# A two-layer graph network: PSUM banks for the queries, a new order on TensorE, and the out-degree counts ahead of the attention loop

## The chip, the cores and the metric

The kernel runs on one core of a Trainium2 chip. The metric is the device time of one execution in microseconds (us); lower is better. TensorE is PE in the profile (its weight loads are PEld), VectorE is DVE, ScalarE is ACT, GpSimd is POOL, and SyncE, which issues the plain transfers, is SP.

## What is computed

3125 nodes with 128 features, 53125 edges sorted by their target `dst`, and 32 features for each edge. Layer 0 is an attention over the edges with 8 heads of 16; layer 1 is a graph convolution that divides by the square roots of the node degrees (in-degree plus out-degree). Cut to what matters here:

```python
Q, K, V = h @ Wq + bq, h @ Wk + bk, h @ Wv + bv        # h = relu(layernorm(x)), 8 heads
scores = sum(Q[dst] * K[src], -1) * scale + (edge_attr @ We + be)
exp_s  = exp(scores - segment_max(scores, dst)[dst])
agg    = segment_sum(exp_s * V[src], dst) / (segment_sum(exp_s, dst) + 1e-10)
x = x + agg @ Wo + bo
deg = segment_sum(1, dst) + segment_sum(1, src)        # the out-degree is the sum over src
x = x + expmap0(segment_sum(h2[src] * dinv[src] * dinv[dst], dst))
```

## The kernel before

**Stages.** First (to about 50 us) all nodes get their Q, K and V, written to tables in memory. Then the attention loop, which the change touches, takes 32 groups of 13 x 128 edges one after the other (about 60 to 971 us). After it comes layer 1, with its own loops.

**One group g of the attention loop.** POOL fetches the K and V rows of the sources, 13 indirect gathers per group into `kv[b]` (L662; two buffers, b = g mod 2). A gather of group g+2 may begin once group g has been weighed (it waits for `s_wv`). SP loads the edge features, the local target numbers `dloc_b` of the edges, spread over all partitions (L515), and a window of 128 query rows `qwin` (L530). PE selects each edge's query row by a product with a one-hot matrix `ST` (L1547): 13 tiles of 128 edges in four chunks `CH` of 4, 4, 4 and 1, into two PSUM banks `ps_q` in turn, so that chunk c waits until DVE has read chunk c-2. `ST` is made by DVE in one instruction (L872, `row_one_hots`). `bias` (L1527, L1531) adds the edge features' part in bank `ps_c`. DVE multiplies queries and keys (L927), sums per head (L933), adds the bias (L944), and then takes a segmented maximum: a scan forward inside a partition (L949), a transposition on PE (L1584), a scan over the partitions (L960), back by PE (L1587), then the same backward (L966 to L968, L1593, L979, L1595, L989 to L991). ACT takes the exponential (L1388), and DVE weighs the V rows (L1004, two instructions; each raises `s_wv`).

**Sums.** `window_sums(g)` on PE adds the weighed rows by target, 13 products with the one-hot matrix `S` (L1559, raises `s_agg`), then moves the carried rows `R` of the group before (L1565) and the carry factor (L1567, raises `s_rc`). DVE's `combine` waits for `s_rc` (L1011 to L1023), and the new rows go through `agn`, L1590, L1378 (ACT), L1600 and L1601 (PE) and L1042 to `x2`. ACT makes most of `S` (L1369 and L1372, `one_hots`), and begins on a buffer once `s_agg` says that its sums are done.

**Out-degree counts.** For each group, inside the loop, DVE makes two one-hot matrices of the sources (`oh_hi`, `oh_lo`, L897), PE multiplies them in 13 small products (L1580) into a part of bank `ps_f`, and DVE adds the result to `od_s` (`add_counts`, L904).

**What sets the order.** Every engine runs its own list of instructions in the order written; semaphores alone tie them. PE's `step(g)` is: query chunks 2 and 3 of group g, sums of group g-1, counts of g, the transpositions of g, the output product of g-1, then chunk 0, half the bias, chunk 1 and the other half of the bias of group g+1. DVE's `step(g)` is `scores(g)`, `combine(g-1)` mixed with the scan of g, the backward scan, `new_rows`, `add_counts`, `factor`, `weigh(g)`. SP waits in each turn for the stored rows of the group before the last.

## Time and profile before

| | us |
|---|---|
| median of 3 runs (1495.43 to 1497.34) | 1495.47 |
| the profiled execution, as timed | 1495.77 |
| its span, first to last instruction | 1493.8 |
| PE busy / DVE busy / ACT busy / POOL busy | 946.3 / 740.5 / 391.2 / 595.5 |
| one group of the attention loop (from its first gather at 408.49 to the next one's at 436.72) | 28.2 |

The profiled execution lies 0.3 us above the median, and 2.0 us of it lie outside the span. How to read the rows further on: a timeline row gives the start in us, the duration, the engine, the line, the operation, the tile written and the tiles read, and in brackets the idle time of the engine before it with what ended that. `<-remote` means that the profile names no instruction for the release; `<-issue` means that the engine waited for nothing that it shows. On PE a row is a time of issue, and its end is modelled. A float32 product shows as two weight loads and two matmuls, so 13 products are x26.

### The profile page before, as it was taken

What the parts mean: (1) busy time and instruction counts of PE and PEld (TensorE: products, weight loads), DVE (VectorE), ACT (ScalarE), POOL (GpSimd) and SP (SyncE); (2) the same over time, 40 slices, a digit from 0 to 9 for tenths busy, and PEclk for the clock granted to TensorE, in tenths of its full rate; (3) what the DMA queues carried; (4) which work ended last, traced back from release to release, by engine and by line L of the source; (5) the groups of instructions that cost most, each with busy time, mean ns of one, the idle gap of its engine ahead of it and who ended that gap; (6) DMA issues with size and microseconds to landing.
All of it is one profiled execution on the core that took longest, in us unless ns stands there. A gap on an engine that the chain in (4) does not pass through costs nothing.

```text
span 1493.8 us, 22198 instructions
## 1 busy us (share of the span) xinstructions
PE 946.3 (63%) x5820; PEld 805.1 (54%) x5820; DVE 740.5 (50%) x2771; ACT 391.2 (26%) x1107; POOL 595.5 (40%) x629
## 2 busy tenths in 40 slices
PE   5355775775775775675675676733757756765775
PEld 2244664664664564564564565622656645654665
DVE  8344544544554554553553553583534544454454
ACT  1502212212212212211311311142323423432341
POOL 0544454354354354354354354005343443444341
PEclk9655566566566566566566566675867877877787
DMA  5622232232232232233232233012011111111111
GB/s 150 178 80 83 87 104 82 84 104 83 81 106 86 77 110 86 72 111 89 71 112 89 70 110 93 6 47 87 26 41 34 40 40 37 37 40 40 33 41 29
DMA packets 87848, 111.23 MB, mean 74 GB/s; under 512 B 20787, under 2 KB 65791, under 8 KB 87807
## 3 DMA queue, kind: packets, MB, share of 16 engines
q0 software_dynamic: 26624, 68.20, 15.8%
q1 hardware_dynamic: 61191, 42.64, 9.9%
q8 instruction: 15, 0.25, 0.1%
q14 instruction: 18, 0.15, 0.0%
HBM read 99.83 MB, written 10.95 MB: 74 GB/s over the span
## 4 chain that ended last, share of the span: by engine, by line
PE 33%; DVE 24%; issue 20%; another core or an unknown queue 19%; DVEq 2%; DMA 1%; SPq 0%; ACT 0%
PE ps_q L1547 10%; PE ps_q L1673 3%; PE ps_q L1698 3%; PE ps_s L1673 3%; PE ps_c L1531 3%; DVE sc L933 2%; DVE wv L1275 2%; PE ps_f L1601 2%; PE ps_f L1600 1%; DVE fwd_reset L1274 1%; DVE prod L927 1%; PE ps_c L1527 1%; DVE oh_lo L897 1%; PE ps_b L1673 1%
## 5 line engine op out<-in xcount | busy, mean ns | idle before, releaser
L662 POOL DMA_INDIRECT kv<-kv_tab,idx x416 | 396.6, 953 | 533.8 <-DVE wv L1004 367.6
L695 POOL DMA_INDIRECT kv<-hs_tab,idx x208 | 198.6, 955 | 335.9 <-PE ps_q L1682 191.6
L1369 ACT ACTIVATE S<-iota,nloc 128x128 f32<-128x128 f32 x384 | 122.0, 389 | 636.1 <-remote 635.0
L1547 PE MATMUL ps_q<-qwin,ST 128*128 128x128 f32 x832 | 207.0, 432 | 19.5 <-DVE prod L927 10.5
L1547 PEld LDWEIGHTS ps_q<-qwin,ST 128*128 128x128 f32 x832 | 187.1, 331 | 20.8 <-DVE prod L927 10.8
L1580 PE MATMUL ps_f<-oh_lo,oh_hi 128*50 128x64 bf16 x416 | 83.4, 301 | 96.2 <-issue 96.0
L927 DVE TENSOR_TENSOR prod<-kv,ps_q 128x512 f32<-128x512 f32 (+1 forms) x128 | 74.6, 583 | 140.2 <-issue 58.8
L1011 DVE TENSOR_SCALAR fb<-ps_c 128x8 f32<-128x8 f32 x32 | 5.3, 166 | 274.3 <-remote 267.3
L1559 PE MATMUL ps_r<-wv,S 128*128 128x137 f32 x832 | 140.1, 341 | 1.8 <-DVE wv L1004 1.8
L1559 PEld LDWEIGHTS ps_r<-wv,S 128*128 128x128 f32 x832 | 140.0, 253 | 2.1 <-DVE wv L1004 2.1
L1580 PEld LDWEIGHTS ps_f<-oh_lo,oh_hi 128*50 128x50 bf16 x416 | 54.2, 172 | 110.4 <-issue 109.4
L1689 PE MATMUL ps_r<-qkv,xt 128*128 128x128 f32 x800 | 95.5, 280 | 5.6 <-issue 5.4
L1689 PEld LDWEIGHTS ps_r<-qkv,xt 128*128 128x128 f32 x800 | 93.6, 196 | 7.6 <-issue 7.6
L1673 PE MATMUL ps_q<-ST,wv 128*128 128x128 bf16 x224 | 48.4, 300 | 63.4 <-issue 47.2
L1587 PE MATMUL ps_b<-ident,c 8*128 8x8 f32 x32 | 7.7, 241 | 127.5 <-DVE c L960 127.5
L1587 PEld LDWEIGHTS ps_b<-ident,c 8*128 8x128 f32 x32 | 5.6, 176 | 142.3 <-issue 142.3
L1673 PE MATMUL ps_s<-ST,wv 128*128 128x128 bf16 x224 | 48.0, 304 | 45.0 <-issue 45.0
L1448 ACT ACTIVATE S<-iota,nloc 128x128 f32<-128x128 f32 x208 | 67.0, 387 | 26.0 <-PE ps_q L1682 26.0
L1531 PEld LDWEIGHTS ps_c<-we,attr_s 128*128 128x128 f32 (+1 forms) x256 | 63.0, 321 | 19.9 <-DMA attr_s<-in_attr 12.1
L1531 PE MATMUL ps_c<-we,attr_s 128*128 128x32 f32 (+1 forms) x256 | 65.8, 378 | 11.8 <-DMA attr_s<-in_attr 11.8
L933 DVE TENSOR_REDUCE sc<-prod 128x32 f32<-128x512 f32 (+1 forms) x128 | 71.5, 579 | 0.0
L1673 PEld LDWEIGHTS ps_q<-ST,wv 128*128 128x128 bf16 x224 | 26.6, 135 | 75.2 <-issue 65.1
(257 smaller groups left out, 1715.6 us busy)
## 6 DMA issues: line engine op xcount, KB each, us to landing
dloc_b<-dloc_tab SPq DMA_DIRECT2D x32, 416.0 KB
kv<-kv_tab,idx POOLq DMA_INDIRECT x416
attr_s<-in_attr SPq DMA_DIRECT2D x32, 192.0 KB
kv<-hs_tab,idx POOLq DMA_INDIRECT x208
kv_tab<-qkv SPq DMA_DIRECT2D x5, 640.0 KB, 4.0
x_tab<-x SPq DMA_DIRECT2D x32, 64.5 KB, 1.7
qwin<-q_tab SPq DMA_DIRECT2D x32, 64.0 KB
xwin<-in_x SPq DMA_DIRECT2D x32, 64.0 KB
```

The source lines that it names most:

```text
L662: pool.indirect_dma_start(out=kv[:, b, t, :], out_offset=None, in_=kv_tab, in_offset=bass.IndirectOffsetOnAxis(ap=idx[:, b, t:t + 1], axis ...
L695: pool.indirect_dma_start(out=kv[:, j, t, 0:D], out_offset=None, in_=hs_tab, in_offset=bass.IndirectOffsetOnAxis(ap=idx[:, j, t:t + 1], ax ...
L927: V.tensor_tensor(prod[:, c % 2, 0:w, :], kv[:, b, t0:t1, 0:D], ps_q[c % 2][:, 0:w * D].rearrange("p (t d) -> p t d", d=D), ALU.mult).then ...
L933: st.mark(V.tensor_reduce(sc[:, :, t0:t1].rearrange("p h t -> p t h"), prod[:, c % 2, 0:t1 - t0, :].rearrange("p t (h d) -> p t h d", d=DH ...
L1369: A.activation(S[:, b, t, :], iota[:], ACT.Abs, bias=nloc[:, g, t:t + 1] if known(g) else nloc[:, bass.ds(g, 1), t:t + 1].rearrange("p g t ...
L1448: A.activation(S[:, j, t, :], iota[:], ACT.Abs, bias=nloc[:, g, t:t + 1] if known(g) else nloc[:, bass.ds(g, 1), t:t + 1].rearrange("p g t ...
L1531: mm = M.matmul(p_bias[:, 4 * H * k:4 * H * k + w], attr_s[0:r, b, k, :], we4[0:r, 0:w], start=False, stop=k == 3)
L1547: mm = M.matmul(ps_q[c % 2][:, (t - t0) * D:(t - t0 + 1) * D], ST[:, b, t, :], qwin[:, b, :], start=True, stop=True)
L1559: mm = M.matmul(ps_r[:, 0:C + 1], S[:, b, t, :], wv[:, t, :], start=(t == 0), stop=(t == T - 1))
L1580: mm = M.matmul(ps_f[0:HI, 3 * D:3 * D + LO], oh_hi[:, b, :, t], oh_lo[:, b, :, t], start=(t == 0), stop=(t == T - 1))
L1673: mm = M.matmul(bank[:, 0:(h1 - h0) * P].rearrange("p (h e) -> p h e", e=P) [:, :, ROW0[t]:ROW0[t] + W], oh_node[:, t, :], oh_key(t)[:, h0 ...
L1689: M.matmul(ps_r[:, 0:D], counts[:, i, :], hs_t[:, i, :], start=(i == 0), stop=False)
```

## The change

- **PSUM.** Four banks hold the four query chunks, `ps_q[0]` to `ps_q[3]`; the old `ps_s` banks are the last two of them. The bias moves into the free part of `ps_q[3]`. A chunk now waits only until DVE has read the same chunk of the group before.
- **PE's order.** `step(g)` begins with the sums of group g-1. The four query chunks of group g+1 stand between and behind the transpositions of g: chunk 0 after L1584's transposition, chunk 1 after the one of `agn`, chunk 2, the whole bias and chunk 3 after the output product.
- **`ST` moves from DVE to ACT.** In place of one DVE instruction, ACT makes two of the same size, the absolute difference and then relu(1 - it), one group earlier than before. SP loads `dloc_b` a group earlier, too.
- **Counts.** The counts of all 32 groups are made before the attention loop, in one PSUM accumulation in bank `ps_r`, and DVE copies the result once. `source_one_hots` and the 13 products leave the loop, and so does `add_counts`.
- **ACT's order.** The third part of `one_hots` goes behind the exponential.

```diff
-        ps_q = [pb(f"ps_q{i}", [P, 512]) for i in range(2)]
-        ps_s = [pb(f"ps_s{i}", [P, 512]) for i in range(2)]
+        ps_q = [pb(f"ps_q{i}", [P, 512]) for i in range(NCH)]
+        ps_s = ps_q[2:]
...
-        p_bias = ps_c[:, 384:384 + HT]
+        p_bias = ps_q[NCH - 1][:, D:D + HT]
+        p_od = ps_r[0:HI, 2 * D:2 * D + LO]
...
-                    wait_apart(sp, s_st, g - 1, (s_base, 1))
+                    wait_apart(sp, s_sta, g - 1, (s_base, 1))
...
-                load_dloc(g, b)
...
+                load_dloc(0, 0)
+                load_dloc(1, 1)
                 load_edges(0, 0)
                 load_edges(1, 1)
+                load_dloc(2, 0)
...
-                with sp.Fori(1, GROUPS // 2) as n:
-                    for b in range(2):
-                        load_edges(2 * n + b, b)
-                        store_nodes(2 * n + b - 2, b)
-                        load_nodes(2 * n + b, b)
+
+                def turn(g, b, more=True):
+                    if more:
+                        load_dloc(g + 1, 1 - b)
+                    load_edges(g, b)
+                    store_nodes(g - 2, b)
+                    load_nodes(g, b)
+
+                with sp.Fori(1, GROUPS // 2 - 1) as n:
+                    turn(2 * n, 0)
+                    turn(2 * n + 1, 1)
+                turn(GROUPS - 2, 0)
+                turn(GROUPS - 1, 1, more=False)
                 store_nodes(GROUPS - 2, 0)
-                sp.wait_ge(s_od, GROUPS)
+                sp.wait_ge(s_od, 1)
...
-            def row_one_hots(g, b):
-
-                dve.wait_ge(s_dlocb[b], 16 * ((g - b) // 2 + 1) if known(g) else (g + (2 - b)) * 8)
-                if not (known(g) and g < 2):
-                    dve.wait_ge(s_qt, NCH * (g - 1))
-                V.tensor_scalar(ST[:, b].rearrange("p t e -> p (t e)"), dloc_b[:, b, :], imj[:, 0:1], None, ALU.is_equal)\
-                    .then_inc(s_st, 1)
...
-            pre.mark(V.memset(od_s[:], 0.0))
             dve.wait_ge(s_reset8, 2 * H)
             dve.wait_ge(s_line, 16)
-            def source_one_hots(g, b, parts=(0, 1)):
-
-                if 0 in parts and not (known(g) and g < 2):
+            def source_one_hots(g, b):
+
+                if not (known(g) and g < 2):
                     dve.wait_ge(s_hist, g - 1)
-                for i in parts:
+                for i in range(2):
...
-            def add_counts(g):
-                dve.wait_ge(s_hist, g + 1)
-                if not (known(g) and g == 0):
-                    dve.wait_ge(s_od, g)
-                V.tensor_tensor(od_s[:], od_s[:], ps_f[0:HI, 3 * D:3 * D + LO], ALU.add).then_inc(s_od, 1)
...
-                if more:
-                    source_one_hots(g + 1, 1 - b, (0,))
...
-                if more:
-                    source_one_hots(g + 1, 1 - b, (1,))
...
-                    row_one_hots(g + 2, b)
...
-                    add_counts(g)
...
-            source_one_hots(0, 0)
...
-                row_one_hots(0, 0)
+                source_one_hots(0, 0)
+                source_one_hots(1, 1)
+                with dve.Fori(1, GROUPS // 2) as n:
+                    source_one_hots(2 * n, 0)
+                    source_one_hots(2 * n + 1, 1)
+                dve.wait_ge(s_hist, GROUPS)
+                V.tensor_copy(od_s[:], p_od).then_inc(s_od, 1)
...
+            def row_one_hots(g, b):
+
+                act.wait_ge(s_dlocb[b], 16 * ((g - b) // 2 + 1) if known(g) else (g + (2 - b)) * 8)
+                if not (known(g) and g < 2):
+                    act.wait_ge(s_qt, NCH * (g - 1))
+                rows = ST[:, b].rearrange("p t e -> p (t e)")
+                A.activation(rows, dloc_b[:, b, :], ACT.Abs, bias=nrow[:]).then_inc(s_sta, 1)
+                act.wait_ge(s_sta, g + 1)
+                A.activation(rows, rows, ACT.Relu, bias=1.0, scale=-1.0).then_inc(s_st, 1)
...
-            def step(g, b, nodes=True, more=True):
+            def step(g, b, nodes=True, more=True, far=True):
+                if far:
+                    row_one_hots(g + 2, b)
                 if more:
-                    one_hots(g + 1, 1 - b, (0, 1))
+                    one_hots(g + 1, 1 - b, (0,))
...
-                    one_hots(g + 1, 1 - b, (2,))
+                    one_hots(g + 1, 1 - b, (1,))
...
-            act.wait_ge(s_nloc, 1)
+                if more:
+                    one_hots(g + 1, 1 - b, (2,))
+
+            act.wait_ge(s_nloc, 2)
...
+                row_one_hots(0, 0)
+                row_one_hots(1, 1)
                 step(0, 0, nodes=False)
-                with act.Fori(0, GROUPS // 2 - 1) as n:
+                step(1, 1)
+                with act.Fori(1, GROUPS // 2 - 1) as n:
+                    step(2 * n, 0)
                     step(2 * n + 1, 1)
-                    step(2 * n + 2, 0)
-                step(GROUPS - 1, 1, more=False)
+                step(GROUPS - 2, 0, far=False)
+                step(GROUPS - 1, 1, more=False, far=False)
...
-                    if c == chunks[0]:
+                    if c == 0:
                         pe.wait_ge(s_st, g + 1)
-                    if not (known(g) and g == 0 and c < 2):
-                        pe.wait_ge(s_prod, NCH * g + c - 1)
+                    if not (known(g) and g == 0):
+                        pe.wait_ge(s_prod, NCH * (g - 1) + c + 1)
                     for t in range(t0, t1):
-                        mm = M.matmul(ps_q[c % 2][:, (t - t0) * D:(t - t0 + 1) * D], ST[:, b, t, :], qwin[:, b, :],
+                        mm = M.matmul(ps_q[c][:, (t - t0) * D:(t - t0 + 1) * D], ST[:, b, t, :], qwin[:, b, :],
                                       start=True, stop=True)
                     mm.then_inc(s_qt, 1)
-            def window_sums(g, b, bias_read=True):
+            def histogram(g, b):
+
+                pe.wait_ge(s_oh, 2 * g + 2)
+                for t in range(T):
+                    mm = M.matmul(p_od, oh_hi[:, b, :, t], oh_lo[:, b, :, t],
+                                  start=known(g) and g == 0 and t == 0, stop=known(g) and g == GROUPS - 1 and t == T - 1)
+                mm.then_inc(s_hist, 1)
+
+            def window_sums(g, b):
...
-                if bias_read:
-                    pe.wait_ge(s_sc, g + 2)
...
+                if nodes:
+                    window_sums(g - 1, 1 - b)
                 if edges:
-                    query(g, b, (2, 3))
-                if nodes:
-                    window_sums(g - 1, 1 - b, edges)
-                if edges:
-
-                    pe.wait_ge(s_oh, 2 * g + 2)
-                    if not (known(g) and g == 0):
-                        pe.wait_ge(s_od, g)
-                    for t in range(T):
-                        mm = M.matmul(ps_f[0:HI, 3 * D:3 * D + LO], oh_hi[:, b, :, t], oh_lo[:, b, :, t],
-                                      start=(t == 0), stop=(t == T - 1))
-                    mm.then_inc(s_hist, 1)
                     pe.wait_ge(s_v1, g + 1)
                     M.transpose(p_v1, f1[:, :, T - 1], ident[:]).then_inc(s_v1T, 1)
-                if edges:
+                    if more:
+                        query(g + 1, 1 - b, (0,))
...
+                    if more:
+                        query(g + 1, 1 - b, (1,))
...
-                    query(g + 1, 1 - b, (0,))
-                    bias(g + 1, 1 - b, (0, 1))
-                    query(g + 1, 1 - b, (1,))
-                    bias(g + 1, 1 - b, (2, 3))
+                    query(g + 1, 1 - b, (2,))
+                    bias(g + 1, 1 - b, (0, 1, 2, 3))
+                    query(g + 1, 1 - b, (3,))
...
+                histogram(0, 0)
+                histogram(1, 1)
+                with pe.Fori(1, GROUPS // 2 - 1) as n:
+                    histogram(2 * n, 0)
+                    histogram(2 * n + 1, 1)
+                histogram(GROUPS - 2, 0)
+                histogram(GROUPS - 1, 1)
+                pe.wait_ge(s_od, 1)
                 bias(0, 0, (0, 1, 2, 3))
-                query(0, 0, (0, 1))
+                query(0, 0, (0, 1, 2, 3))
```

How this moves the instructions: on PE, in the steady part of the loop, before (`ps_q0` and `ps_q1` are the two query banks, L1559 the sums, L1580 the counts, L1587 to L1593 transpositions):

```order
L1547 MATMUL ps_q0<-qwin,ST 128x128 x4
L1545 REGISTER_ALU
L1547 MATMUL ps_q1<-qwin,ST 128x128
L1553 REGISTER_ALU
L1554 REGISTER_ALU
L1559 MATMUL ps_r<-wv,S 128x137 x13
L1565 MATMUL ps_c<-R,shift 128x137
L1567 MATMUL ps_c<-facd,isf 128x8
L1576 ISA
L1580 MATMUL ps_f<-oh_lo,oh_hi 50x64 x13
L1584 MATMUL ps_b<-ident,f1 8x128
L1587 MATMUL ps_b<-ident,c1 128x8
```

The counts stand between the sums and the first transposition, and the query chunks ahead of the sums. The same place after the change (the sums are L1581, the queries L1561, the transposition of `c1` is L1598):

```order
L1581 MATMUL ps_r<-wv,S 128x137 x13
L1585 MATMUL ps_c<-R,shift 128x137
L1587 MATMUL ps_c<-facd,isf 128x8
L1593 REGISTER_ALU
L1594 MATMUL ps_b<-ident,f1 8x128
L1553 ISA
L1559 ISA
L1561 MATMUL ps_q0<-qwin,ST 128x128 x4
L1598 MATMUL ps_b<-ident,c1 128x8
L1601 MATMUL ps_f<-ident,agn 128x128
L1559 REGISTER_ALU
L1561 MATMUL ps_q1<-qwin,ST 128x128 x4
```

The counts are gone, and chunks 0 and 1 of the next group now stand among the transpositions. On DVE, in `combine`, before (L1011 reads the product of L1567, L872 makes `ST`, L1023 adds the sums):

```order
L1011 TENSOR_SCALAR fb<-ps_c 128x8
L1012 COPY R<-ps_c 128x1
L860 TENSOR_SCALAR shift<-imj,delta 128x128
L1016 TENSOR_TENSOR R<-ps_c,fb 128x136
L864 TENSOR_TENSOR S<-dloc,iota 128x128
L872 TENSOR_SCALAR ST<-dloc_b,imj 128x1664
L1023 TENSOR_TENSOR R<-R,ps_r 128x137
```

And after:

```order
L1006 TENSOR_SCALAR fb<-ps_c 128x8
L1007 COPY R<-ps_c 128x1
L874 TENSOR_SCALAR shift<-imj,delta 128x128
L1011 TENSOR_TENSOR R<-ps_c,fb 128x136
L878 TENSOR_TENSOR S<-dloc,iota 128x128
L1017 TENSOR_TENSOR R<-R,ps_r 128x137
```

The instruction that made `ST` has left the path from the release of `combine` to the addition.

## Rows read from the trace of the kernel before

**Rows 1.** Head of the page: span.

```profile
span 1493.8 us, 22198 instructions
```

**Rows 2.** Waits, 90 to 1000 us: total us, times, longest us.

```profile
ACT S L1369 <- remote: 635.0, 30, 21.4
POOL kv L662 <- DVE wv L1004: 367.6, 30, 17.0
DVE fb L1011 <- remote: 267.3, 30, 9.3
```

**Rows 3.** Timeline, one group of the attention loop, 408 to 428 us.

```profile
408.49 0.95 POOL L662 DMA_INDIRECT kv<-kv_tab,idx  x1 [12.11 <-DVE wv L1004]
...
414.13 4.10 PE L1559 MATMUL ps_r<-wv,S 128*128 128x137 f32 x26
...
418.39 0.38 PE L1567 MATMUL ps_c<-facd,isf 8*128 8x8 f32 x2
...
422.67 0.28 PE L1580 MATMUL ps_f<-oh_lo,oh_hi 128*50 128x64 bf16 x1 [1.06 <-issue]
...
423.37 0.28 PE L1580 MATMUL ps_f<-oh_lo,oh_hi 128*50 128x64 bf16 x1 [0.42 <-issue]
...
423.59 0.95 POOL L662 DMA_INDIRECT kv<-kv_tab,idx  x1 [0.30 <-issue]
...
427.08 0.17 DVE L1011 TENSOR_SCALAR fb<-ps_c 128x8 f32<-128x8 f32 x1 [8.81 <-remote]
427.14 1.28 ACT L1369 ACTIVATE S<-iota,nloc 128x128 f32<-128x128 f32 x4 [21.27 <-remote]
```

**Rows 4.** Timeline, the same group after the release, 427 to 437 us.

```profile
427.83 1.08 DVE L872 TENSOR_SCALAR ST<-dloc_b,imj 128x1664 f32<-128x1664 bf16 x1
...
431.26 0.38 PE L1593 MATMUL ps_b<-ident,bx 128*8 128x128 f32 x1 [0.49 <-DVE bx L968]
...
433.77 1.92 PE L1547 MATMUL ps_q<-qwin,ST 128*128 128x128 f32 x8
...
434.48 0.20 DVE L904 TENSOR_TENSOR od_s<-od_s,ps_f 50x64 f32<-50x64 f32 x1
...
435.62 0.75 PE L1527 MATMUL ps_c<-be_r,ones_row 1*128 1x104 f32 x2
...
436.30 1.06 PE L1531 MATMUL ps_c<-we,attr_s 128*128 128x32 f32 x4
...
436.72 0.94 POOL L662 DMA_INDIRECT kv<-kv_tab,idx  x1 [12.18 <-DVE wv L1004]
```

**Rows 5.** Timeline, group 31's step, in which no gather runs, 948 to 954 us.

```profile
948.66 4.76 PE L1559 MATMUL ps_r<-wv,S 128*128 128x137 f32 x26
...
954.00 0.17 DVE L1011 TENSOR_SCALAR fb<-ps_c 128x8 f32<-128x8 f32 x1 [2.26 <-PE ps_c L1567]
```

**Rows 6.** Timeline, the step of group 1, 99 to 118 us.

```profile
99.40 0.94 POOL L662 DMA_INDIRECT kv<-kv_tab,idx  x1 [17.00 <-DVE wv L1004]
...
115.80 1.28 ACT L1369 ACTIVATE S<-iota,nloc 128x128 f32<-128x128 f32 x4 [18.41 <-remote]
...
117.86 0.17 DVE L1011 TENSOR_SCALAR fb<-ps_c 128x8 f32<-128x8 f32 x1 [9.34 <-remote]
```

**Rows 7.** Timeline, the start of the attention loop, 58 to 99 us.

```profile
58.86 0.52 DVE L897 TENSOR_TENSOR oh_hi<-hi_f,rep_hi 128x650 bf16<-128x650 bf16 x1 [8.15 <-ACT bwd_reset L1407]
59.30 0.61 DVE L897 TENSOR_TENSOR oh_lo<-lo_f,rep_hi 128x832 bf16<-128x832 bf16 x1
...
81.45 0.95 POOL L662 DMA_INDIRECT kv<-kv_tab,idx  x1 [0.30 <-issue]
...
86.42 0.69 DVE L927 TENSOR_TENSOR prod<-kv,ps_q 128x512 f32<-128x512 f32 x1 [11.95 <-remote]
...
87.89 1.76 PE L1580 MATMUL ps_f<-oh_lo,oh_hi 128*50 128x64 bf16 x13
...
97.42 1.96 DVE L1004 TENSOR_TENSOR wv<-kv,wv 128x1024 f32<-128x1024 f32 x2 [0.20 <-ACT wv L1388]
```

More of the change, by code:

```diff
@@ L185, in build @@
         dloc_b = sb("dloc_b", [P, 2, GE], BF16)
+        nrow = sb("nrow", [P, 1])
         lo_f = sb("lo_f", [P, GROUPS, T], BF16)
@@ L359, in build @@
         s_stp = sem("s_stp")
+        s_sta = sem("s_sta")
         s_st = sem("s_st")
@@ L843, in _ @@
             V.tensor_scalar(nloc[:], dloc[:], -1.0, None, ALU.mult).then_inc(s_nloc, 1)
+            V.tensor_scalar(nrow[:], imj[:, 0:1], -1.0, None, ALU.mult).then_inc(s_nloc, 1)
             V.tensor_scalar(part_reset[:], part_reset[:], BIG, None, ALU.mult).then_inc(s_part, 1)
@@ L916, in mask8, with scores @@
                 return col3(tile, g).unsqueeze(1).to_broadcast([P, H, T])
-            def scores(g, b, st, more):
+            def scores(g, b, st):
                 def product(c):
@@ L927, in product @@
                     V.tensor_tensor(prod[:, c % 2, 0:w, :], kv[:, b, t0:t1, 0:D],
-                                    ps_q[c % 2][:, 0:w * D].rearrange("p (t d) -> p t d", d=D), ALU.mult).then_inc(s_prod, 1)
+                                    ps_q[c][:, 0:w * D].rearrange("p (t d) -> p t d", d=D), ALU.mult).then_inc(s_prod, 1)
                 def per_head(c):
@@ L1055, in step @@
                 if edges:
-                    scores(g, b, A, more)
+                    scores(g, b, A)
                 if nodes:
@@ L1064, in step @@
                     edge_one_hots(g + 1, 1 - b, s_S, TA)
-                    row_one_hots(g + 1, 1 - b)
                 if edges:
```

## The prediction

> **What bounds the kernel now.** I read the list of waits first, then the timeline of one group of the attention loop, then the places where that pattern is broken. The waits [rows 2] show three engines that stand still together: POOL for 367.6 us until a group is weighed, and ACT for 635.0 us and DVE for 267.3 us on a release that no instruction accounts for ("remote"). One group shows where these lie [rows 3]. POOL's 13 gathers run from 408.49 to 424.54, and PE issues the sums at 414.13 and the carry product L1567 at 418.39, modelled to end at 418.77. DVE's `combine` reads that product, yet it starts at 427.08, and ACT, which waits for the sums, at 427.14. Meanwhile PE issues its small products one at a time, 0.70 us apart (422.67, 423.37). So what PE has finished reaches the others some 8.3 us late, and it reaches them 18.6 us after the first gather (408.49 to 427.08), 2.5 us after the last one has ended.
>
> Two other places say on what this hangs. In group 31's step no gather runs, and DVE starts 5.3 us after the sums do, not 12.9 us [rows 5]. In the step of group 1 ACT was released 16.4 us and DVE 18.5 us after the first gather [rows 6]: the release can come a little before the gathers end, but not much. I conclude that a step is a loop of two legs. **Leg 1** runs from the first gather to the release of `combine`, 18.6 us, and its length is that of the gathers. **Leg 2** runs from the release through the scans to the weighing, which lets POOL begin the next gathers: 427.08 to 436.72 [rows 3, 4], 9.6 us. Together 28.2 us, 31 times, some 875 of the span of 1493.8 us [rows 1]. Work inside leg 1 is covered; work in leg 2, or ahead of the loop, is paid.
>
> **Part 1: the counts ahead of the loop.** Inside the loop they are nearly free: the two one-hots (0.52 and 0.61 us [rows 7]) and the 13 products lie in leg 1, and only the addition L904 (0.20 us [rows 4]) lies in leg 2. Moved ahead they are all on the path, since bias, queries and the first step now stand behind them on PE and DVE. Without gathers 13 such products take 1.76 us with the modelled end of the last [rows 7]; I take 1.6 us per group, more than DVE's 1.13 us. The first gathers run until 82.4 (81.45 + 0.95), and PE's releases were held until 86.42 [rows 7], and DVE idled 11.95 us on a remote release there. So I let only 2 of the 32 groups through by 86.4, and the other 30 end at 86.4 + 30 x 1.6 = 134.4. Then come the bias (0.75 + 2 x 1.06 = 2.9 us) and two query chunks (2 x 1.92) [rows 4], so DVE's second product starts at 141.1. From there to the first weighing it was 97.42 - 86.42 = 11.0 us [rows 7], which I keep: 152.1 in place of 97.42, **+54.7 us**. The ends: if nothing is held, the counts start at 59.4 and end at 110.6, which gives +30.9; with no group through by 86.4 and 1.76 us each, +63.
>
> **Part 2: `ST` goes to ACT.** L872 (1.08 us [rows 4]) leaves DVE in leg 2. ACT does two instructions of that size. The widest ACT row at hand is four one-hots in 1.28 us, 512 columns [rows 3]; by columns 1664 come to 4.2 us each at most, 8.3 us for two, against some 21 us in which ACT idles before L1369 [rows 3]. They are used a group later. I cost them at nothing; were they in leg 2, they would cost up to 8 us a group, but the order puts them ahead of the wait for the sums. SP's earlier `dloc_b` moves a transfer inside leg 1 and is not waited for.
>
> **Part 3: PE's new order.** Chunk 0 (1.92 us [rows 4]) now stands behind the transposition of `f1`. In leg 1 PE can issue it while the others wait, so it costs nothing. Chunk 1 is issued behind the transposition of `agn`, which comes in leg 2, and right ahead of the transposition L1593 on which DVE waits: +1.92 us, less the 0.49 us that PE idled there, less what L872's going gives back. So leg 2 changes by +1.92 - 0.49 - 1.08 - 0.20 = +0.15 us; the ends are -1.28 (if chunk 1 is hidden entirely) and +0.64 (if PE's idle time takes up none of it). I take **0 +- 5 us** for the loop; over 31 steps the ends are -40 and +20. Chunk 2, the bias and chunk 3 follow the output product (1.92 + 2.9 + 0.5 = 5.3 us, chunk 3 being one tile of 13). From chunk 0 of before at 433.77 that is 439.1, so that the sums start 2.4 us after the first gather (436.72 [rows 4]) in place of 5.6 us (408.49 to 414.13 [rows 3]).
>
> **Do the sums then get through?** This decides. Between the first gather and the sums PE had before the change chunk 1 (8 passes), part of the bias, and chunks 2 and 3 (10), some 22 passes; now it has most of the bias and chunk 3, some 9. That is some 13 passes fewer, and 3.2 us. But 3.2 us earlier is not enough, if the rate of the reports is what is short: at 0.70 us for one, 12 us of leg 1 carry 17. ACT's 7 instructions have come into leg 1 as well. I take it that the release still comes with the end of the gathers.
>
> A release is prompt where nothing disturbs it: in [rows 5] it is 5.3 us from the first sum, all 30 passes included. The Trainium skill, "TensorE: Matmul & The Clock Gate", section "The cost: per-tile semaphore tail", puts one increment some 56 ns behind its matmul. By that rule `combine` would start at 418.8 in place of 427.08, and the loop after the change would be the third rival below; the trace disagrees by 8.3 us while gathers run.
>
> **Sum:** 1495.8 (the profiled execution) + 54.7 + 0 = 1550.5, and 0.3 less against the median: **1550 us**.
>
> **Rivals.** *First, faster: the release comes before the gathers end.* Mechanism: with fewer passes ahead of it, `s_rc` reaches DVE by, say, 14 us after the first gather; `combine` and the scan of L960 run under the gathers, and at their end only the backward part is left. It decides if the release comes more than 1 us before the 18.6 us. For it: [rows 6], where ACT was released at 16.4 us, with no transfers by SP in that stretch. Against it: the whole of what follows needs further reports. Price: of the 4.2 us from L1011 to L1593 (427.08 to 431.26 [rows 3, 4]) some 3 us, 30 times 3 = 90: 1550 - 90 = 1460; with all 4.2 us, 1424.
>
> *Second, slower: PE cannot issue chunk 0 under cover.* Then it runs in leg 2, ahead of the transposition of `c1`: 1.92 x 31 = 60, 1610 us. For it: in [rows 3] PE issues its small products only 0.70 us apart while the others wait, as if its queue were full. Against it: it still advances by one every 0.70 us, and chunk 0 has 8 passes and over 9 us. The Trainium skill, same page, section "Architectural detail: the array is 16x 32x32, not 1x 128x128", gives TensorE a queue of 64; sums, carry, `f1` and chunk 0 make 78 entries by it, so 14 would have to be freed first. The trace agrees in so far as the issue slows down in that stretch, and at 0.70 us each the 14 are freed within leg 1, so the forecast has no price for it.
>
> *Third, much faster: the lateness goes away altogether*, because it hung on the order of PE's work and not on the gathers. Then the sums start 2.4 us after the first gather, the release follows 5.3 us later [rows 5], and leg 2 takes its 9.6 us: 17.3 us a step, just over the 16.4 us of 13 gathers (408.49 to 424.54 and one pause of 0.30 [rows 3]). 31 x 10.9 = 338 saved: 1212. Against it: POOL would then gather without a break, and releases are late just while it gathers.
>
> **Chances.** Forecast 0.60 (its own range 1515 to 1575), first rival 0.21, second 0.11, third 0.08. The range reaches down to the middle of the first rival, 1440, and up to 1590; left out are the third, the second and the far end of the first, about 0.2. A measurement of this kernel tells 0.2%, 3 us, from no change. Faster: 0.29; slower: 0.60 and 0.11 less a little, 0.69; within 0.2%: 0.02.
>
> **What would show it.** In the profile after: the last count product at about 134 us and the first L1004 at about 152; a step of the loop still 28 us, with DVE's first instruction of `combine` released by "remote" 18 to 19 us after the first gather; chunk 1 in 1.9 us ahead of the transposition of `bx`. The forecast is wrong if the step is 25 us or less (the release was not tied to the gathers, or got through early), or if the counts end before 115 (the hold did not apply to them).

## Result: slower by 2.2% in the recorded comparison, faster by 5.8% in another

| | before | after |
|---|---|---|
| median (runs) | 1495.45 us (4) | 1527.86 us (4, 1524.74 to 1533.82) |
| the profiled execution, as timed | 1495.77 | 1524.91 |
| its span | 1493.8 | 1523.1 |

The ratio is 1.0222, with a 95% interval of 1.0193 to 1.025: slower, clear of noise, and by about 2%. 1550 us was forecast, with a range of 1440 to 1590.

The experiments then met a second condition of the hardware, which has to be told first, because every number below depends on it. The delay of PE's releases that [rows 3] show is not always there. The kernels were run on several occasions, each time together with the kernel before. On some occasions the kernel before takes 1495 to 1511 us and PE's releases come late while POOL gathers. On others the same kernel takes 1043 to 1044 us and they come at once. All runs of one occasion, those of the kernel before among them, agreed in this. I call the two **with the delay** and **without**; comparisons of times hold inside one occasion only. The recorded comparison is one with the delay. Without it the unaltered changed kernel takes 984.15 us beside 1044.06 us (below).

**The profile after, with the delay.** The list of waits, 90 to 1000 us (total us, times, longest us), answers [rows 2]:

```profile
POOL kv L675 <- DVE wv L999: 406.3, 30, 70.4
DVE fb L1006 <- remote: 350.9, 28, 13.5
...
ACT S L1365 <- remote: 172.4, 28, 10.7
```

DVE waits longer for the release of `combine` than before (350.9 us for 267.3 us), since it comes to that wait earlier. ACT waits less (172.4 us for 635.0 us), since it now makes `ST` and waits for its input, and since what it waits for is released earlier, as the group below shows. The first row holds one wait of 70.4 us: POOL stands still during the counts. The start of the loop in the timeline (start, duration, in brackets the idle time before) answers [rows 7]:

```profile
59.31 0.52 DVE L902 TENSOR_TENSOR oh_hi<-hi_f,rep_hi 128x650 bf16<-128x650 bf16 x1 [9.42 <-issue]
...
80.70 0.95 POOL L675 DMA_INDIRECT kv<-kv_tab,idx  x1 [0.30 <-issue]
...
85.69 0.52 DVE L902 TENSOR_TENSOR oh_hi<-hi_f,rep_hi 128x650 bf16<-128x650 bf16 x1 [18.62 <-remote]
...
86.79 45.17 PE L1569 MATMUL ps_r<-oh_lo,oh_hi 128*50 128x64 bf16 x377 [17.90 <-DVE oh_lo L902]
...
132.00 0.22 DVE L1172 COPY od_s<-ps_r 50x64 f32<-50x64 f32 x1 [1.93 <-PE ps_r L1569]
...
137.07 0.69 DVE L926 TENSOR_TENSOR prod<-kv,ps_q 128x512 f32<-128x512 f32 x1 [4.86 <-PE ps_q L1561]
...
150.06 1.96 DVE L999 TENSOR_TENSOR wv<-kv,wv 128x1024 f32<-128x1024 f32 x2 [0.33 <-ACT wv L1394]
```

DVE stands still for 18.62 us in the middle of the counts, until 4.0 us after the last of the first gathers has ended, as forecast. 29 of the 32 groups (377 = 29 x 13 products) follow it. The first weighing is at 150.06 in place of 97.42. A group in the loop, beside [rows 3] and [rows 4]:

```profile
785.98 0.94 POOL L675 DMA_INDIRECT kv<-kv_tab,idx  x1 [11.96 <-DVE wv L999]
...
788.33 5.77 PE L1581 MATMUL ps_r<-wv,S 128*128 128x137 f32 x26
...
790.75 1.68 ACT L1376 ACTIVATE ST<-dloc_b,nrow 128x1664 f32<-128x1664 bf16 x1 [5.50 <-DMA dloc_b<-dloc_tab]
...
792.46 1.59 ACT L1378 ACTIVATE ST<-ST 128x1664 f32<-128x1664 f32 x1
...
794.26 0.38 PE L1587 MATMUL ps_c<-facd,isf 8*128 8x8 f32 x2
...
800.28 1.28 ACT L1365 ACTIVATE S<-iota,nloc 128x128 f32<-128x128 f32 x4 [6.22 <-remote]
...
801.00 0.94 POOL L675 DMA_INDIRECT kv<-kv_tab,idx  x1 [0.30 <-issue]
...
804.39 0.17 DVE L1006 TENSOR_SCALAR fb<-ps_c 128x8 f32<-128x8 f32 x1 [13.29 <-remote]
...
806.88 1.91 PE L1561 MATMUL ps_q<-qwin,ST 128*128 128x128 f32 x8
...
808.58 0.42 PE L1606 MATMUL ps_b<-ident,bx 128*8 128x128 f32 x1
...
813.95 0.95 POOL L675 DMA_INDIRECT kv<-kv_tab,idx  x1 [12.00 <-DVE wv L999]
```

The sums start 2.35 us after the first gather, in place of 5.64 us, and the carry product is issued 8.3 us after it, in place of 9.9 us. DVE gains almost nothing by it: `combine` starts 18.4 us after the first gather, where it was 18.6 us. The product is now almost 10 us old when DVE learns of it. ACT does gain. It waits for the sums alone, which PE issues just ahead of the carry product, and starts at 800.28, 14.3 us after the first gather and with one gather still to come. In the kernel before it started together with DVE, 18.7 us after the first gather (427.14 in [rows 3]). But ACT is not on the path. Leg 2 is 9.56 us (804.39 to 813.95), where it was 9.64 us.

**Where the time went**, by the weighings of the groups in both timelines (their first and last, 97.42 and 961.12 before, 150.06 and 988.91 after). The counts cost 52.6 us ahead of the loop. The loop is 24.9 us shorter: 10.8 us in 27 steady steps (0.4 each), 3.2 us in the first step and 10.8 us in the last three. Layer 1 is 1.5 us longer. 52.6 - 24.9 + 1.5 = 29.2 us; the spans, 1493.8 and 1523.1, differ by 29.3, which is rounding. In the first and the last steps the release did come before the end of the gathers. The last burst:

```profile
951.26 0.95 POOL L675 DMA_INDIRECT kv<-kv_tab,idx  x1 [9.57 <-DVE wv L999]
...
963.36 0.17 DVE L1006 TENSOR_SCALAR fb<-ps_c 128x8 f32<-128x8 f32 x1 [6.99 <-remote]
...
966.31 0.95 POOL L675 DMA_INDIRECT kv<-kv_tab,idx  x1 [0.31 <-issue]
```

12.1 us after the first gather, while the last gather still starts at 966.31.

### The profile page after: what moved, and what is told of

Same layout as the page of the kernel before. It is cut to its first block, busy times and chain, and to the rows that moved or that the text cites. A ratio compares the mean times of both kernels' runs of the same rounds, so it can differ in the third digit from the quotient of the medians.

```text
span 1523.1 us, 22133 instructions
## 1 busy us (share of the span) xinstructions
PE 904.4 (59%) x5820; PEld 793.5 (52%) x5820; DVE 708.6 (47%) x2708; ACT 499.1 (33%) x1171; POOL 595.3 (39%) x629
## 4 chain that ended last, share of the span: by engine, by line
another core or an unknown queue 26%; DVE 26%; PE 25%; issue 17%; DVEq 2%; DMA 1%; ACT 1%; SPq 0%; ACTq 0%
PE ps_q L1693 6%; PE ps_q L1561 4%; DVE sc L932 3%; PE ps_r L1569 3%; PE ps_q L1718 3%; DVE wv L999 3%; DVE prod L926 2%; DVE wv L1271 2%; PE ps_f L1614 2%; DVE fwd_reset L1270 2%; PE ps_f L1613 1%; DVE ST L1270 1%; PE ps_r L1581 1%; PE ps_f L1601 1%
## 5 line engine op out<-in xcount | busy, mean ns | idle before, releaser
L1598 PE MATMUL ps_b<-ident,c 8*128 8x8 f32 x32 | 7.7, 239 | 314.2 <-DVE c L955 296.3
L1006 DVE TENSOR_SCALAR fb<-ps_c 128x8 f32<-128x8 f32 x32 | 5.3, 166 | 384.2 <-remote 350.9
L1365 ACT ACTIVATE S<-iota,nloc 128x128 f32<-128x128 f32 x384 | 122.1, 389 | 184.9 <-remote 172.4
L1561 PE MATMUL ps_q<-qwin,ST 128*128 128x128 f32 x832 | 181.2, 382 | 0.0
L1598 PEld LDWEIGHTS ps_b<-ident,c 8*128 8x128 f32 x32 | 5.6, 175 | 319.4 <-issue 319.4
L1561 PEld LDWEIGHTS ps_q<-qwin,ST 128*128 128x128 f32 x832 | 163.0, 287 | 0.8
L1581 PE MATMUL ps_r<-wv,S 128*128 128x137 f32 x832 | 160.0, 374 | 1.8 <-DVE wv L999 1.8
L1581 PEld LDWEIGHTS ps_r<-wv,S 128*128 128x128 f32 x832 | 159.9, 284 | 2.0 <-DVE wv L999 2.0
L1376 ACT ACTIVATE ST<-dloc_b,nrow 128x1664 f32<-128x1664 bf16 x32 | 53.8, 1682 | 230.2 <-DMA dloc_b<-dloc_tab 138.3
L1693 PE MATMUL ps_q<-ST,wv 128*128 128x128 bf16 x448 | 61.3, 302 | 105.4 <-issue 92.3
L1693 PEld LDWEIGHTS ps_q<-ST,wv 128*128 128x128 bf16 x448 | 46.0, 136 | 124.7 <-issue 108.9
L1569 PE MATMUL ps_r<-oh_lo,oh_hi 128*50 128x64 bf16 x416 | 50.3, 299 | 35.9 <-DVE oh_lo L902 32.5
L1474 ACT COPY xt<-ps_q 128x512 f32<-128x512 f32 x64 | 32.9, 600 | 117.2 <-PE ps_q L1693 105.1
L1569 PEld LDWEIGHTS ps_r<-oh_lo,oh_hi 128*50 128x50 bf16 x416 | 49.5, 170 | 36.6 <-DVE oh_lo L902 33.0
```

Of the source, the lines that this page charges most:

```text
L1365: A.activation(S[:, b, t, :], iota[:], ACT.Abs, bias=nloc[:, g, t:t + 1] if known(g) else nloc[:, bass.ds(g, 1), t:t + 1].rearrange("p g t ...
L1376: A.activation(rows, dloc_b[:, b, :], ACT.Abs, bias=nrow[:]).then_inc(s_sta, 1)
L1561: mm = M.matmul(ps_q[c][:, (t - t0) * D:(t - t0 + 1) * D], ST[:, b, t, :], qwin[:, b, :], start=True, stop=True)
L1569: mm = M.matmul(p_od, oh_hi[:, b, :, t], oh_lo[:, b, :, t], start=known(g) and g == 0 and t == 0, stop=known(g) and g == GROUPS - 1 and t ...
L1581: mm = M.matmul(ps_r[:, 0:C + 1], S[:, b, t, :], wv[:, t, :], start=(t == 0), stop=(t == T - 1))
L1693: mm = M.matmul(bank[:, 0:(h1 - h0) * P].rearrange("p (h e) -> p h e", e=P) [:, :, ROW0[t]:ROW0[t] + W], oh_node[:, t, :], oh_key(t)[:, h0 ...
```

## Experiments

### First occasion: the counts, and SP's loads (without the delay)

The kernel before took 1043.92 us here (13 runs), not 1495 us. This is where the second condition showed itself; no expectation written for this occasion had foreseen it, so their times are not met.

**Part 1 alone**, in the kernel before:

```diff
-                    add_counts(g)
+                source_one_hots(0, 0)
...
+                dve.wait_ge(s_hist, GROUPS)
+                V.tensor_copy(od_s[:], p_od).then_inc(s_od, 1)
```

> The kernel before with part 1 alone: the counts ahead of the loop, PE's and ACT's order and the banks as before. After the change the first weighing came 52.6 us later (97.42 to 150.06), and that should repeat here. Theory 'end of the gathers' (the release of `combine` comes 18.5 us after the first gather whatever is queued): the loop loses only the addition L904, 31 x 0.2 = 6 us; in all 1495.5 + 52.6 - 6 = 1542 us. Theory 'shared' (while gathers run, the instructions that all engines have in that stretch hold one another up, so that fewer of them release `combine` earlier): the counts stood behind the carry product on PE, but two one-hots of DVE and 26 weight loads and products leave the stretch; the release should move to 15 to 18 us, and the time to 1460 to 1530 us.

Measured: 1094.04 us, ratio 1.0481 (1.0463 to 1.0498).

**The counts left out** of the kernel before (no one-hots of the sources, no products, no addition; zeros in `od_s`):

> The kernel before, the out-degree counts left out altogether (zeros instead). It prices what the counts cost inside the loop. 'End of the gathers': 0.2 us a group, 1495.5 - 6 = 1489 us. 'Shared': the release comes at 15 to 18 us in place of 18.5, and the time is 1410 to 1480 us.

Measured: 1043.53 us, ratio 0.9996 (0.9986 to 1.0005). So the counts inside the loop cost nothing that can be measured, not even the 6 us of the additions, and the two runs together price the phase ahead of the loop at 50.5 us. Its timeline shows one step of the old order without the delay:

```profile
427.42 0.94 POOL L662 DMA_INDIRECT kv<-kv_tab,idx  x1 [3.61 <-DVE wv L1000]
...
433.19 4.73 PE L1553 MATMUL ps_r<-wv,S 128*128 128x137 f32 x26
...
438.09 0.38 PE L1561 MATMUL ps_c<-facd,isf 8*128 8x8 f32 x2
...
438.51 0.17 DVE L1007 TENSOR_SCALAR fb<-ps_c 128x8 f32<-128x8 f32 x1 [2.08 <-PE ps_c L1561]
...
448.21 0.94 POOL L662 DMA_INDIRECT kv<-kv_tab,idx  x1 [4.37 <-DVE wv L1000]
```

`combine` starts 0.42 us after the issue of the carry product, not 8.7 us after it as in [rows 3], with the same order of instructions up to there and the same gathers beside it. What bounds the step here is a chain through PE: query chunks, sums, `combine`, scans, weighing, 20.5 us on the average, and POOL waits some 4 us in each.

**The counts back in the loop** of the changed kernel, parts 2 and 3 kept:

```diff
+                    add_counts(g)
...
-                histogram(0, 0)
...
+                    for t in range(T):
+                        mm = M.matmul(ps_f[0:HI, 3 * D:3 * D + LO], oh_hi[:, b, :, t], oh_lo[:, b, :, t],
```

> The changed kernel with the counts put back into the loop, as before the change (the one-hots behind the scores, the 13 products behind the sums, an addition a group), parts 2 and 3 kept. The 52.6 us ahead of the loop go. 'End of the gathers': 1527.9 - 52.6 + 6 = 1481 us. 'Shared': the 28 additional instructions push every release back to 18.5 us, and the early releases of the first and last steps (9.9, 14.9 and 12.1 us) are lost, so the loop gives back most of the 25 us it had won: 1490 to 1505 us.

Measured: 955.90 us, ratio 0.9186 (0.9125 to 0.9247). Parts 2 and 3 are worth 8.1% without the delay.

**SP's loads left out** from group 2 on, in the changed kernel (the data of groups 0 and 1 are used again, so the scores are not the reference's):

> The changed kernel without SP's loads of dloc_b, attr_s and qwin for groups 2 to 31 (the data of groups 0 and 1 are used again). In the changed kernel the release of `combine` came 17.0 to 18.5 us after the first gather where SP made all its loads, 14.9 and 12.1 us in the last two bursts of gathers, where it made fewer, and 9.9 us in the first, where it made none. 'End of the gathers': no change, 18.5 us, 1528 us. 'Shared' or 'SP's transfers': some 15 of SP's instructions and 4 transfers fewer in each burst, release at 10 to 14 us, step 23 to 25 us, 1400 to 1450 us.

Measured: 983.98 us, ratio 0.9422 (0.9404 to 0.9441). It says nothing on the delay, since there was none; beside the next run it says that the loads cost nothing without it.

### Second occasion: the changed kernel itself (without the delay)

> The changed kernel unaltered, beside the kernel before. In the first four runs the kernel before took 1044 us in place of 1495 us, and PE's releases came without delay. If the comparison is again one without the delay: the counts ahead of the loop cost 1094.0 - 1043.5 = 50.5 us, so 955.9 + 50.5 = 1006 us against 1044 us, faster by 3.6%. If it is one with the delay: 1528 us against 1495 us, and the theories 'end of the gathers' and 'shared' both expect that.

Measured: 984.15 us beside 1044.06 us, ratio 0.9421 (0.939 to 0.9452). 1006 us was expected from the price of the phase; it is 22 us less, because the loop of the changed kernel without the counts is also shorter than with them (weighing to weighing 523.7 us for 543.9 us). The waits of 150 to 600 us:

```profile
POOL kv L675 <- issue: 102.3, 336, 0.3
DVE prod L926 <- DMA kv<-kv_tab,idx: 96.4, 39, 4.9
```

POOL waits for nothing but its own pause of 0.3 us between two gathers, and DVE waits for gathered rows. The step of 17.07 us (groups 2 to 28) is that of 13 gathers, a few of which take longer than the usual 0.95 us (2.39 us below). In the timeline of one step:

```profile
386.44 0.38 PE L1587 MATMUL ps_c<-facd,isf 8*128 8x8 f32 x2
...
388.16 0.69 DVE L926 TENSOR_TENSOR prod<-kv,ps_q 128x512 f32<-128x512 f32 x1 [3.36 <-DMA kv<-kv_tab,idx]
...
391.39 0.14 DVE L1006 TENSOR_SCALAR fb<-ps_c 128x8 f32<-128x8 f32 x1
...
399.78 2.39 POOL L675 DMA_INDIRECT kv<-kv_tab,idx  x1 [0.30 <-issue]
...
402.47 0.94 POOL L675 DMA_INDIRECT kv<-kv_tab,idx  x1 [0.30 <-issue]
```

The carry product is issued 5 us before DVE comes to it, so sums that stood on the path before the change stand beside it now.

**ACT's first part of `S` behind the copy of `agT`,** and its second behind the exponential:

```diff
-                if more:
-                    one_hots(g + 1, 1 - b, (0,))
                 if nodes:
                     agg_copy(g - 1)
                 if more:
-                    one_hots(g + 1, 1 - b, (1,))
+                    one_hots(g + 1, 1 - b, (0,))
                 carry_factor(g)
                 weights(g)
                 if more:
-                    one_hots(g + 1, 1 - b, (2,))
+                    one_hots(g + 1, 1 - b, (1, 2))
```

> The changed kernel with ACT's first part of the one-hots `S` moved behind the copy of `agT`, so that ACT runs nothing between the sums and the release of `combine`. Without the delay: within 1% of the changed kernel, since ACT has idle time. With it: 'end of the gathers' expects the release at 18.5 us as in the changed kernel, 'shared' expects it at 13 to 16 us, as the five instructions of ACT no longer stand between the sums and the carry product.

Measured: 985.73 us (2 runs), no difference from the changed kernel. What it was made for, the delay, was not there.

### Third occasion: parts 2 and 3 undone one at a time (with the delay, before 1507.57 us)

**`ST` on DVE again:**

```diff
+                if far:
+                    row_one_hots(g + 3, 1 - b)
```

> The changed kernel with `ST` made by DVE's one instruction again (behind the one-hots `S` in `combine`, still a group ahead), so part 2 alone undone. Without the delay of PE's releases the changed kernel took 984 us and its step 17.07 us, which is the gathers' own 13 x 1.25 us and a short pause. If the gathers bound the step (third rival of the prediction), 1.1 us more on DVE is mostly covered: 984 to 995 us. If DVE's path bounds it, 31 x 1.1 = 34 us: 1018 us.

Measured: 1575.89 us, ratio 1.0454 (1.0433 to 1.0475). A step of it, in the timeline:

```profile
672.24 0.94 POOL L675 DMA_INDIRECT kv<-kv_tab,idx  x1 [13.25 <-DVE wv L1007]
...
690.91 0.17 DVE L1014 TENSOR_SCALAR fb<-ps_c 128x8 f32<-128x8 f32 x1 [13.63 <-remote]
...
691.66 1.08 DVE L886 TENSOR_SCALAR ST<-dloc_b,imj 128x1664 f32<-128x1664 bf16 x1
...
701.35 0.95 POOL L675 DMA_INDIRECT kv<-kv_tab,idx  x1 [13.16 <-DVE wv L1007]
```

**PE's queries and bias where they stood before:**

```diff
+                    query(g, b, (2, 3))
                 if nodes:
                     window_sums(g - 1, 1 - b)
...
-                        query(g + 1, 1 - b, (1,))
```

> The changed kernel with PE's query chunks and the bias where they stood before the change (chunks 2 and 3 ahead of the sums, 0 and 1 behind the output product), the four banks, `ST` on ACT and the counts ahead kept, so part 3's order alone undone. Without the delay: if the order is what shortened the step from 20.5 to 17.1 us, it returns to 19 to 20.5 us, since the product of chunk 2 waits for PE in the stretch behind the weighing: 1045 to 1080 us. If the banks or `ST` did it: 984 to 1000 us.

Measured: 1524.66 us, ratio 1.0113 (1.0093 to 1.0133):

```profile
640.12 0.94 POOL L675 DMA_INDIRECT kv<-kv_tab,idx  x1 [11.28 <-DVE wv L999]
...
658.87 0.17 DVE L1006 TENSOR_SCALAR fb<-ps_c 128x8 f32<-128x8 f32 x1 [8.16 <-remote]
...
667.27 0.95 POOL L675 DMA_INDIRECT kv<-kv_tab,idx  x1 [11.24 <-DVE wv L999]
```

In both the release of `combine` stays near where it was, 18.7 us after the first gather (672.24 to 690.91, 640.12 to 658.87), for 18.4 us in the changed kernel. Leg 2 changes: 10.44 us with `ST` on DVE and 8.40 us with the old order on PE. It is 0.1 us longer in every second step, so these two go with the 9.46 us of the changed kernel's next step (832.42 to 841.88) and not with the 9.56 us above. So `ST`'s going gave 1.0 us a step, and chunk 1 on the path took 1.1 us of it back. The expectations of these two runs were written for the other condition, so their numbers are not met.

The old order of PE also shows what the new one does to the releases. With it ACT is released 18.4 to 18.9 us after the first gather in every burst (18.8 us in the step above), with the new one, in the changed kernel, after 12.2 to 15.1 us in all steady steps but one (16.4 us). For `combine` this counts mainly at the ends of the loop: in the first and the last three steps the new order is 9.4 us shorter in all, in the 27 others it is 14.5 us longer (27.75 us a step for 27.21 us). The loop is 838.8 us with the new order and 833.7 us with the old one. So with the delay part 3 is a small loss. The ratios to the kernel before (1.0113 without it, 1.0222 with it) say the same, but they come from two occasions, and layer 1, which is the same in both kernels, differs by 5.9 us between them (540.1 us for 534.2 us). How the 3.4 us a step that parts 2 and 3 bring without the delay divide between them was not measured.

### Fourth and fifth occasion: a version that beats both, and fewer gathers

**The counts hidden in the loop:** the changed kernel with the counts back in the loop, their DVE part ahead of the product of chunk 2:

```diff
+                    if c == 1:
+                        if not (known(g) and g == 0):
+                            add_counts(g - 1)
+                        if more:
+                            source_one_hots(g + 1, 1 - b)
                     if c + 1 < NCH:
                         product(c + 1)
```

> A version that may beat both: the changed kernel with the counts in the loop, the 13 products behind the sums on PE, and DVE's one-hots and the addition of the counts put ahead of the product of chunk 2, where DVE waits for the gathered rows. Without the delay: the loop keeps the changed kernel's step of 17.1 us and loses the 47 us ahead of it: 984 - 47 = 937 us, against 956 us with the one-hots behind the scores. With the delay: 'end of the gathers' expects 1481 us, 'shared' 1490 to 1505 us, before 1495 us.

Measured without the delay: 939.87 us beside 1043.79 us, ratio 0.8997 (0.8968 to 0.9027). 937 us was expected. In its timeline the three instructions stand where DVE would wait for rows, and the wait that is left there is 0.60 us:

```profile
307.96 0.20 DVE L910 TENSOR_TENSOR od_s<-od_s,ps_f 50x64 f32<-50x64 f32 x1
308.08 0.51 DVE L903 TENSOR_TENSOR oh_hi<-hi_f,rep_hi 128x650 bf16<-128x650 bf16 x1
308.52 0.60 DVE L903 TENSOR_TENSOR oh_lo<-lo_f,rep_hi 128x832 bf16<-128x832 bf16 x1
...
309.72 0.69 DVE L933 TENSOR_TENSOR prod<-kv,ps_q 128x512 f32<-128x512 f32 x1 [0.60 <-DMA kv<-kv_tab,idx]
```

The step is 17.06 us, that of the changed kernel, with the first weighing at 82.50. The same kernel on the fifth occasion:

> The version with the counts hidden in the loop once more, for the other condition of the chip if it shows. With the delay: no counts phase ahead (-52.6 us), the step of the changed kernel, at most 0.3 us more: 1528 - 53 + 0 to 10 = 1475 to 1485 us against 1495 us of before. Without it: 940 us against 1044 us, as measured.

Measured with the delay: 1496.22 us beside 1510.56 us, ratio 0.9908 (0.9886 to 0.9931). It beats the kernel before under both conditions, here by 0.9%. The time expected, 1475 to 1485 us, was not met. The kernel before itself took 15 us more than in the recorded comparison. And the loop takes 856.7 us in place of the changed kernel's 838.8: none of its 27 steady steps has an early release (all 18.55 to 18.78 us after the first gather), where the changed kernel has seven. So with the delay the counts do not seem free in the loop (17.9 us between these two traces, which are of two occasions), but cheaper than ahead of it (the first weighing comes at 99.29 in place of 150.06).

**Six gathers of 13** from group 2 on, in the changed kernel (the other tiles keep old rows, so the sums are not the reference's):

```diff
+FEW = (2, 2, 1, 1)
...
-                    for t in range(t0, t1):
+                    for t in range(t0, t1 if known(g) else t0 + FEW[c]):
```

> The changed kernel with 6 of the 13 gathers of each group from group 2 on (the other tiles keep the rows of groups 0 and 1). If PE's releases are delayed (the kernel before at about 1500 us): the last gather then ends 5 x 1.255 + 0.95 = 7.2 us after the first, and if the release hangs on the end of the gathers, `combine` starts 9.6 us after the first gather in place of 18.5 us, the step falls to about 19 us, and layer 1 stays as it is: 1250 to 1270 us. If the delay has nothing to do with the gathers, 1528 us stays. If nothing is delayed (before at 1044 us): the step of 17.07 us was the gathers', so it falls to the path of DVE, which is busy about 15 us a step: 984 less 31 x 1.5 to 2 us, 920 to 940 us.

Measured with the delay: 1225.62 us beside 1510.56 us, ratio 0.8116 (0.806 to 0.8171). The expected 1250 to 1270 us are missed by 24 us, since the step is 17.3 us and not 19. The first three rows are of one of three bursts inside the loop in which the carry product comes early, the others of a usual one:

```profile
304.86 0.94 POOL L676 DMA_INDIRECT kv<-kv_tab,idx  x1 [9.57 <-DVE wv L1000]
...
308.27 0.38 PE L1588 MATMUL ps_c<-facd,isf 8*128 8x8 f32 x2
...
313.63 0.17 DVE L1007 TENSOR_SCALAR fb<-ps_c 128x8 f32<-128x8 f32 x1 [3.64 <-remote]
...
426.81 0.94 POOL L676 DMA_INDIRECT kv<-kv_tab,idx  x1 [10.14 <-DVE wv L1000]
...
433.05 0.95 POOL L676 DMA_INDIRECT kv<-kv_tab,idx  x1 [0.30 <-issue]
...
433.80 0.38 PE L1588 MATMUL ps_c<-facd,isf 8*128 8x8 f32 x2
...
435.62 0.17 DVE L1007 TENSOR_SCALAR fb<-ps_c 128x8 f32<-128x8 f32 x1 [3.80 <-PE ps_c L1588]
...
444.35 0.94 POOL L676 DMA_INDIRECT kv<-kv_tab,idx  x1 [10.36 <-DVE wv L1000]
```

The release follows the gathers: it comes 8.8 us after the first (9.6 us expected) in place of 18.4 us, 1.6 us after the last has ended, and 1.8 us after the issue of the carry product where it was 10 us. That it hangs on the gathers and not on the product is seen where the product is issued at 308.27, 3.4 us after the first gather: the release comes 8.8 us after the gather there, too. So with the delay the gathers set the length of leg 1, as the prediction had it.

**What holds it while they run** is open. The theory "shared" (the number of instructions of all engines in the burst) does not order the early releases: counted up to the release, the last bursts held 142 instructions (12.1 us, changed kernel), 145 (17.2 us, `ST` on DVE) and 173 (12.2 us, counts hidden). SP's transfers order them only in part. In the three kernels with PE's new order the first burst has none of them, and it released after 9.9, 10.0 and 5.9 us; the last has fewer than elsewhere (12.1, 17.2 and 12.2 us). But the last burst but one has all of them and released after 14.9, 18.7 and 17.3 us. And with PE's old order the first burst, with no transfer of SP, released only after 18.5 us, in the kernel before [rows 6] and in the run with the old order alike. There the sums are issued 5.2 us after the first gather, in the three others at most 1.8 us after it. So what is issued early in a burst gets through early, at least at the ends of the loop. That is not all either: ACT's releases in the steady steps come after 12.2 to 16.4 us in the changed kernel, after 15.8 to 18.8 us with `ST` on DVE and after 12.3 to 18.7 us with the counts hidden, all three with the new order. No run takes these apart. The last run, on a sixth occasion, was to decide on SP's transfers:

> The changed kernel without SP's loads of dloc_b, attr_s and qwin for groups 2 to 31 once more (the data of groups 0 and 1 are used again). So far, with the delay, a burst of gathers in which SP makes none of its transfers released `combine` after 5.9 to 10.0 us, one with fewer after 12.1 to 17.3 us, all others after 17.0 to 18.8 us, in three kernels; the number of instructions of all engines does not order them (173 in the burst that took 12.2 us, 142 in the one that took 12.1 us, 145 in the one that took 17.2 us). If SP's transfers beside the gathers carry the delay, every burst releases after 6 to 10 us, and the step falls to 17 to 20 us: 1190 to 1290 us beside about 1500 us of before. If the end of the gathers alone carries it, 18.5 us and about 1530 us stay. If nothing is delayed in this run, 984 us as before, and the question stays open.

Measured: 985.86 us beside 1043.32 us, so without the delay, and the question stays open as that text says.

## Why the prediction was right, and where it was not

**Part 1** held. 54.7 us were forecast, 52.6 us came. The hold until the end of the gathers ended at 85.69 (86.42 assumed), 3 groups were through by then (2 assumed), and the others took 45.17 / 29 = 1.56 us each (1.6 assumed). Without the delay nothing is held: on the second occasion the counts run in one piece from 60.38 and the first weighing is at 128.44, which is the lower end that the prediction gave for that case (+30.9, 128.3). The price is not the lower one, though: the kernel without the counts weighs first at 78.72 there, so the phase costs 50 to 53 us under both conditions.

**Part 2** held: `ST` on ACT costs nothing, and putting it back costs 1.0 us of leg 2 a step (1.08 us assumed). The two instructions take 1.68 and 1.59 us, not up to 4.2 us each. One reading was wrong, at no cost: ACT does wait for SP's `dloc_b` (5.50 us at 790.75), in time in which nothing waits for ACT.

**Part 3** held in leg 2: +0.15 us a step was forecast for both parts together, -0.08 us came, and chunk 1 took 1.1 us of the path (1.92 - 0.49 = 1.43 us assumed).

**"I take it that the release still comes with the end of the gathers"** is the step that was mis-sized. For `combine` it held in most of the 27 steady steps, though in seven of them the release came one or two steps of 0.7 us earlier, and not in the first burst and the last two. For ACT, which waits for the sums alone, it did not hold: its releases came 1 to 4 us before the end of the gathers in nearly all steps. The term for the loop, 0 +- 5 us with ends of -40 and +20, measured -24.9 us. With 54.7 in place of 52.6, 0 in place of -24.9 and nothing for layer 1's 1.5 us, the sum of 1550.5 us lies 25.6 us above the profiled execution (1524.91 us), and the forecast 22 us above the median. The first rival was thus right in some steps and wrong in the others: the sums do get through early, and the carry product behind them mostly does not.

**The third rival** described the other condition. It put the step without any lateness at 17.3 us, and 17.07 us came. That the numbers agree is partly luck: its 17.3 us are a chain of sums, release and leg 2, with the gathers' 16.4 us just under it, and it is the gathers that bound the step. Its time of 1212 us is wrong all the same, since layer 1 is shorter without the delay, too (532.7 us behind the last weighing of the kernel before with it, 330 us of the changed kernel without), and since the kernel before is then fast as well. It was wrong in the cause: no order of PE's work takes the delay away, as [rows 3] and the step of the first occasion show with one and the same order.

**What I missed** is that a cause which I took for a property of the kernel was a condition of the run. Nothing in one trace could tell, but [rows 3] had a sign: no instruction of the program asks for a release 8.3 us late, or for products 0.70 us apart. That the recorded comparison fell under the condition of the trace that the forecast was made from was luck. Without the delay the same two kernels take 1044.06 and 984.15 us, and the forecast is wrong in size and in direction.

## What to carry to other kernels

A step that is bound by gathers can take in work for nothing wherever an engine waits for rows, and work moved out of it is paid in full; look for the wait before moving anything ahead of a loop. Where "remote" waits lengthen every step and the producing instruction ended long before, time the unaltered kernel again on another occasion before building on it: the sign of a change can hang on it. Keep a version that is better under both conditions rather than one that is best under one.

## What the runs showed of the hardware

With the delay, `combine`, which waits for PE's carry product, starts 2.3 to 2.9 us after the last of 13 gathers has ended in most steps of five kernels, and 1.45 to 1.67 us after the last of 6 in every burst but the first, however long the product has been done. The gathers do not shut everything out while they run: in the changed kernel ACT is released by the sums 12.2 to 15.1 us after the first gather, up to 3.8 us before the last one ends, in all steady steps but one. Without the delay `combine` starts 0.42 us after the issue of the product, with the same gathers beside it. The same kernel takes 1495 to 1511 us or 1043 to 1044 us, a factor of 1.43 to 1.45, and both conditions were met on runs that name the same chip (984.15 us on the second occasion, 1575.89 us on the third). What brings the condition on no run shows. PE's mean granted clock is lower with the delay (0.672 for the changed kernel, 0.81 without), which fits an engine that stands still more; whether it is cause or effect was not tested.
